# A perceiver layer on one Trainium2 core: query weights first, query products ahead of the spreads, first key step by kinds

## What is computed

```python
xn = _layernorm(x)                                   # 256 x 512
q = (xn @ Wq + bq) * scale; q = _fq_sym(q, axis=-1)  # rounded per head
k = ctx @ Wk + bk;          k = _fq_sym(k, axis=-1)  # 4096 x 512, rounded per head and token
```

## Time and profile before

| | |
|---|---|
| three executions | 581.07, 582.43, 583.52 us |
| the profiled execution: its span | 582.8 us |
| the profiled execution: device time of its own | none shown beside the span |
| TensorE busy | 531.9 us, 91% |
| VectorE busy | 457.6 us, 79% |
| ScalarE busy | 364.7 us, 63% |
| GpSimd busy | 28.4 us, 5% |
| loaded from HBM | 75.27 MB, 131 GB/s over the span |

### The profile page before, as it was taken

How to read it: one execution, slowest core, us unless ns; L and a number is a source line. 1 busy time by engine, 2 the same in 40 slices (tenths; PEclk the granted TensorE clock), 3 DMA queues, 4 the chain that set the end, 5 groups by cost and what they waited for, 6 DMA issues and landing times. The chain is left out here.

```text
span 582.8 us, 10649 instructions
## 1 busy us (share of the span) xinstructions
PE 531.9 (91%) x4283; PEld 333.8 (57%) x4286; DVE 457.6 (79%) x858; ACT 364.7 (63%) x431; POOL 28.4 (5%) x28
## 2 busy tenths in 40 slices
PE   3999999999899999999998788699999899996995
PEld 2444555543566656665665565488884565652582
DVE  2599999966899989998999797401593889878995
ACT  5624656464799889988998788400343753586342
POOL 0300000000300200030005100000000000000000
PEclk9999999999999999999998788899999999997999
DMA  8723300042345435553556459603938204300000
GB/s 319 264 74 87 130 1 1 0 142 85 119 148 182 165 107 176 166 168 112 160 177 241 170 165 432 265 1 95 319 163 341 106 0 180 111 0 0 2 2 36
DMA packets 20145, 78.84 MB, mean 135 GB/s; under 512 B 2176, under 2 KB 3200, under 8 KB 16896
## 3 DMA queue, kind: packets, MB, share of 16 engines
q1 hardware_dynamic: 20096, 78.16, 37.8%
HBM read 75.27 MB, written 0.79 MB: 131 GB/s over the span
## 5 line engine op out<-in xcount | busy, mean ns | idle before, releaser
L1122 DVE CUSTOM_DVE_ANT_0 arena<-ps,arena 128x1024 f32<-128x1024 f32 x128 | 152.5, 1220 | 16.2 <-issue 7.7
L1530 ACT ACTIVATE arena<-arena,small 128x4096 int16<-128x4096 f32 x32 | 121.5, 3798 | 2.5 <-DVE small L1135 2.4
L600 PE MATMUL ps<-arena 128*128 128x512 f16 x384 | 100.1, 380 | 0.0
L641 PE MATMUL ps<-small,arena 128*128 128x128 bf16 x1024 | 81.7, 225 | 8.1 <-DVE arena L1142 4.8
L566 PE MATMUL ps<-arena 128*128 128x512 f16 x384 | 85.2, 379 | 1.2 <-DVE arena L1053 1.2
L641 PEld LDWEIGHTS ps<-small,arena 128*128 128x128 bf16 x1024 | 61.1, 100 | 17.8 <-issue 6.9
L1537 ACT ACTIVATE arena<-ps 128x512 int32<-128x512 int32 x96 | 56.9, 593 | 21.7 <-PE ps L641 21.3
L815 PE MATMUL ps<-arena 128*128 128x256 f32 (+1 forms) x288 | 67.3, 397 | 0.7 <-ACT arena L1619 0.7
L815 PEld LDWEIGHTS ps<-arena 128*128 128x128 f32 x288 | 55.7, 194 | 11.8 <-issue 3.3
L566 PEld LDWEIGHTS ps<-arena 128*128 128x128 f16 x384 | 37.2, 98 | 43.6 <-issue 1.5
L657 PEld LDWEIGHTS ps<-arena 128*128 128x128 f16 x1024 | 43.0, 97 | 30.1 <-issue 8.2
(11 more groups left out here) (172 smaller groups left out, 729.5 us busy)
## 6 DMA issues: line engine op xcount, KB each, us to landing
arena<-key_scales SPq DMA_DIRECT2D x64, 512.0 KB, 5.0
arena<-in_ctxT SPq DMA_DIRECT2D x8, 1024.0 KB, 6.8
arena<-in_wg SPq DMA_DIRECT2D x4, 1024.0 KB, 7.2
arena<-in_wo SPq DMA_DIRECT2D x2, 2048.0 KB, 11.6
arena<-in_wu SPq DMA_DIRECT2D x4, 1024.0 KB, 6.9
arena<-in_wd SPq DMA_DIRECT2D x4, 1024.0 KB, 5.8
arena<-in_wuq SPq DMA_DIRECT2D x1, 3072.0 KB, 24.9
arena<-in_wkr SPq DMA_DIRECT2D x1, 2048.0 KB, 13.9
```

The source lines that it names most:

```text
L600: last = pe.matmul(ps[:, bank, :], wv16[wpart][:, k, g * P:(g + 1) * P], ctx16[cpart][:, k, tok], start=(k == 0 and i == 0), stop=(k == KC ...
L641: last = pe.transpose(ps[:, bank, :].bitcast(BF16)[:, b * P:(b + 1) * P], p16[u % 2][:, (8 * q + b) * P:(8 * q + b + 1) * P].bitcast(BF16) ...
L1122: dve.tensor_tensor_reduce(sc[:, u % 2, i * SCW:(i + 1) * SCW], ps[:, 2 * (n % 2):2 * (n % 2) + 2, :].rearrange("p a b -> p (a b)"), skb[: ...
L1530: act.activation(p16[u % 2], sc[:, u % 2, :], ACT.Exp, bias=ebias[:, u % 2:u % 2 + 1], scale=sq[:, i:i + 1], accum_out=rsum[:, u:u + 1]).t ...
```

## The change

1. SP issues the query weights third, ahead of the key weights.
2. VectorE, not ScalarE, copies the two turned latents out of PSUM, ahead of its first `split_max`.
3. TensorE's order becomes: turned latents, first half of the query products, spread 0, second half, spread 1, step 0 of the keys with spread 2 inside it, spread 3, then steps 1 to 7 as before.
4. Step 0 of the keys is done by kinds: 16 products high x high over all four banks once both high parts are there, then spread 2, then 16 of each other kind as the low parts come.
5. GpSimd, not ScalarE, makes the high part of the key weights, ahead of its work on the queries. A semaphore of its own marks it, and `high_done(e)` picks between the two.

```diff
+            sp.dma_start(wq_sb, wq).then_inc(ld_wq, 16)
             sp.dma_start(wk_stage, wk).then_inc(ld_wkv[0], 16)
             sp.dma_start(stage[0], ctx[:, :, 0:TOK]).then_inc(ld_ctx[0], 16)
             sp.dma_start(idb[:, :], identb).then_inc(ld_const, 16)
             sp.dma_start(bv_sb[:, :], bvT).then_inc(ld_const, 16)
-            sp.dma_start(wq_sb, wq).then_inc(ld_wq, 16)
...
+        def high_done(e):
+            return (xhi, e) if e else (xhi_first, 1)
...
+            def project_first_keys():
+
+                for i, (cpart, wpart) in enumerate(((0, 0), (0, 1), (1, 0))):
+                    if i == 0:
+                        pe.wait_ge(*high_done(0))
+                        pe.wait_ge(*high_done(1))
+                    else:
+                        pe.wait_ge(xlo, i)
+                    for c in range(4):
+                        for k in range(KC):
+                            last = pe.matmul(ps[:, c, :], ctx16[cpart][:, k, c * P:(c + 1) * P], wk16[wpart][:, k, :],
+                                             start=(k == 0 and i == 0), stop=(k == KC - 1 and i == 2))
+                        if i == 2 and c % 2:
+                            last.then_inc(kproj, 1)
+                    if i == 0:
+                        spread_max(2)
...
             turn_latents()
+            project_queries(0)
             spread_max(0)
+            project_queries(1)
             spread_max(1)
-            project_queries(0)
-            project_queries(1)
-            spread_max(2)
-            for j in range(STEPS):
+            project_first_keys()
+            spread_max(3)
+            for j in range(1, STEPS):
...
-                dve.wait_ge(xhi, e + 1)
+                dve.wait_ge(*high_done(e))
...
             normalize(x_sb, xn, 0)
+            for t in range(QT):
+                dve.wait_ge(s_xnT, t + 1)
+                dve.tensor_copy(xnT[:, :, t * P:(t + 1) * P],
+                                ps[:, 4 + t, :].rearrange("p (k a) -> p k a", k=KC)).then_inc(s_xnTe, 1)
...
+            def high_part_of_weights():
+                src, (high, low) = extent(0)
+                pool.wait_ge(xs, 1)
+                pool.tensor_scalar(high, src, xscale[:, 0:1], 0.0, ALU.mult, ALU.add).then_inc(xhi_first, 1)
+
+            high_part_of_weights()
             bias_queries()
...
-            store_latents()
-            high_part(0)
             high_part(1)
```

More of the change, by code:

```diff
@@ L166, in build @@
         xst = sem("scale_steps")
-        xm, xr_, xs, xhi, xlo = (sem(n) for n in (
-            "bound_done", "bound_spread", "split_scale", "high_parts", "low_parts"))
+        xm, xr_, xs, xhi_first, xhi, xlo = (sem(n) for n in (
+            "bound_done", "bound_spread", "split_scale", "high_part_by_pool", "high_parts", "low_parts"))
         ld_x, ld_wq, ld_const, ld_bq, ld_bk, ld_id = (sem(n) for n in (
@@ L1464, in std @@
                 act.activation(rstd[:, :], rstd[:, :], ACT.Sqrt).then_inc(s_std, 1)
[L1466 to L1470, removed]
             def store_projected_queries():
```

## The result

The changed kernel took 588.43 us (median of 4, 586.66 to 591.29) against 582.97 before (median of 4): a ratio of 1.0102, 95% interval 1.0067 to 1.0137. The time lies within 0.1 us of the forecast of 588.4. The difference of 5.5 us is 0.5 less than the forecast's 6.0, since the median of before, 582.43 with three executions, is 582.97 with four. The profile shows that this closeness is partly luck, so the terms matter more than the sum.

The account below looks back on a forecast made before the run. VectorE was taken to set the pace up to key step 2, so a late third spread delays the end. 4.3 us for that delay plus 1.7 for the clock gave 6.0 on 582.43: 588.4 us, range 585.0 to 591.0.

Parts of the forecast that it names:

- What bounds the kernel: Up to key step 2 (45.66 us) VectorE sets the pace; a late third spread delays the end one for one.
- Parts 1 and 2: Early weights, VectorE copies, new TensorE order: queries from 10.6, second spread at 20.46 with open tail, keys from 23.8.
- the price of the reorder is zero: Opening weight and context loads: issuing the same transfers in another order costs nothing, with 5 us of cover.
- The term for the queries: Sixteen query instructions on TensorE take the same 9.64 us as before; bounds 6.9 and 13.8.
- Part 3: GpSimd's high part of the key weights takes 2.25 us, at a price of zero.
- the late case: GpSimd's upper bound, 5.9 us: the two low parts are delayed by 2.1 us, costing 0.6.
- Part 4: Key step 0 by kinds: third spread at 27.25 instead of 22.96, 4.3 us later, carried on to step 2.
- its two terms: Third spread's delay: keys start at 23.8 after the second spread's open tail, then 16 products of 0.216 stand ahead.
- Part 5: TensorE's 3.0 us gap before the keys drops its clock for some 3.3 us, adding 1.7 us; bounds 0 and 3.5.
- more falls: Rival, chance 0.09: new waits at 40.0 and before step 2 also drop the clock, +1.7 us, 590.1.
- its span is 0.4 above the median: Profiled execution of the kernel before: its 582.8 us span was set against the 582.43 median.
- the rival with no fall: Rival, chance 0.22: TensorE's clock does not fall in the gap before the keys; 4.3 us alone, 586.7.

Follow-up runs that it names:

- e7: Kernel before, with only the third spread moved behind the first half of key step 0 (24 products): 586.69 us, ratio 1.0089.
- a0: The changed kernel run once more, no edit: 587.50 us, ratio 1.0108.
- e5: Changed kernel with TensorE's idle times before the keys and in step 1 filled by products whose result is not used: 587.58 us, ratio 1.0095.
- e10: Changed kernel with the high part of the key weights back on ScalarE instead of GpSimd: 587.95 us, ratio 1.0097.
- e8: Kernel before with only the query weights loaded third and the turned latents copied by VectorE: 584.27 us, ratio 1.0043.
- e1: Changed kernel with the second spread half way through the second half of the query products: 585.34 us, ratio 1.0040.
- e3: Changed kernel with ScalarE's third bound ahead of its high part, third spread ahead of the key products, kinds within each half: 585.62 us, ratio 1.0043.
- e9: Changed kernel with kinds within halves, spreads between query products, third behind 4 key products, key weights loaded before query weights, first spread before queries: 581.99 us, ratio 0.9990.

## Why the prediction was right, point by point

**What bounds the kernel.** Right. A delay of the third spread goes to the end one for one (e7), and the stretch from step 2 to the end is 536.8, 536.0, 536.6 and 539.4 us in the four profiles with the changed front (the changed kernel, a0, e5, e10) against 537.1, 536.8 and 535.2 in three of before. Over the first 106 us behind step 2 these seven agree to 0.1 us. No delay is taken back there. The 539.4 is the fall of the clock in late stages that is told under e5.

**Parts 1 and 2.** Right in mechanism and nearly in size: queries from 10.54 (forecast 10.6), second spread at 20.22 (20.46), keys from 23.61 (23.8). The step "the price of the reorder is zero" holds only together with the new order on TensorE; e8 shows +2.0 without it. The term for the queries, 9.64 us for sixteen, is one draw of a scatter: 9.80 and 9.79 busy in two profiles of before, 8.50 in the third. That its 0.86 and 0.43 are the two levels of the clock is argued from the distances alone: the granted clock of the view reads 1.00 from 13.3 to 18.0 in the kernel before, where the starts are 0.86 apart.

**Part 3.** Right. GpSimd took 1.98 us (2.25 taken), and e10 moves nothing in the front. Two of its numbers are loose, and neither decided anything: the 1.12 us is not "alone", since VectorE works beside it (L1122, 128x1024 out of PSUM, 1.22 us at 148.82), and by the prediction's own numbers the late case costs 23.8 + 4.7 - 27.7 = 0.8, not 0.6.

**Part 4.** Right: third spread at 27.06 (27.25), evacuation 0/0 at 32.66 (33.1), step 2 at 49.57 (50.0), so 3.9 instead of 4.3. Of its two terms e1 gives back part of the first (1.7 us of step 2's start, for a spread that is 1.7 us earlier) and e3 shows the other from a second side: 16 key products ahead of the third spread, and the low parts behind a late second scale.

**Part 5.** Wrong. The step that failed is "the gap is longer than the one that fell, so I take a fall": the clock stayed at 1.00 behind the 3.0 us in the changed kernel, a0 and e10. It fell behind the shorter second idle time, where TensorE waits for VectorE anyway; of the rival "more falls" this half came true, without its price. Measured for this term in the median: nothing (e5 against a0, 0.1 us). The forecast's 1.7 has no counterpart in the changed kernel. The size was not unreasonable: in e3 the fall came in front of the key products and took 1.4 us of TensorE's time. What the prediction could not have from one row of each kind is whether it comes.

**The sum against the median.** The step "its span is 0.4 above the median" was wrong: it compared a span with device times. With the 1.8 us that lie around it, the profiled execution of before was 1.6 above the median, which is why the two traces stand only 3.6 apart. The sum itself was of differences and did not use that step, but a reader who had checked it against the two traces would have found it 2.4 too high. What is placed: by the mean of four profiles with the changed front (49.57, 48.89, 48.85 and, in e5, 49.17: 49.1) and three of before (45.66, 45.60, 44.23: 45.2), step 2 starts 4.0 later; forecast for this 4.3. What the medians say: 5.5 in the first comparison, 4.5 in a0's, and 5.3 in e5's and e10's. The 0.5 to 1.5 us between are not placed. Behind step 2 the four profiles have a mean of 537.2 us and the three of before 536.4; these 0.8 come from e10 alone, and few profiles cannot tell whether they belong to the change. The forecast filled the rest with a fall of the clock in front of the third spread that no profile of the changed kernel shows, so its 588.4 is closer to 588.43 than its reasons deserve; the rival with no fall, 586.7, describes the traces better.

## What to carry to other kernels

Before moving work ahead of a small product that starts a chain over several engines, write down what hides that chain's tail now: here the place of a spread that takes 0.2 us of TensorE's time decided 4 us, because engines run in order and the chain behind it (maximum, scale, high part, low part) had been hidden behind the very work that was moved ahead of it. Starting one input of a pipeline earlier gains nothing until the slowest ring is also started earlier. And compare a profiled execution with the median on the same measure, device time with device time.

## What the runs showed of the hardware

An idle time of 3.0 us between dense query products and dense key products left TensorE's granted clock at 1.00 in three profiles (the changed kernel, a0, e10). In e3 the same time, with one short spread inside it, was followed by 0.50. An idle time of 2.4 us, 15 us later, was followed by the lower level in the same three profiles (0.60 to 0.63 over the next 4.3 to 4.6 us), and the same 2.38 us in e1 and 2.71 us in e7 by 1.00. Length alone does not tell which idle time costs, and one profile of a kernel does not price it. The Trainium skill ("TensorE: Matmul & The Clock Gate", Why this matters for your kernels) warns of idle time between bursts of matmuls because the clock can go back. The falls in the changed kernel and in e3 agree with that in kind; the idle times without a fall show that the warning does not settle a single case.

GpSimd's 128x1024 multiply-add on the queries took 2.96 us beside VectorE's low part in the kernel before and 1.05 apart from it in the changed one. In e9, where GpSimd starts 0.02 us ahead of the low part, it keeps its 1.06 and VectorE pays, 3.18 instead of 2.35; in the kernel before, where the low part started 0.54 us ahead, GpSimd paid most of it. The Trainium skill ("GPSIMD Engine Reference", Specifications) names SBUF interfaces that GpSimd shares with VectorE, and contention with VectorE instructions of two SBUF inputs, as the low part is. The traces agree, and show that either side can pay.
